# Routed and local attention on one core: token load order, routing logits, token-major local output, halved last sequence

## What is computed

```python
xn = layernorm(x)
s  = attn(xn, Wq, Wk, Wv)     # 8 heads, causal relu(QK^T)/512 times V, summed over heads, plus xn
g  = silu(ffn(xn, ...))
return x + s * g
```

```python
summed = scattered_routed_outputs + local_out
counts = (how many groups chose the token) + 1
ffn    = summed / counts
```

## Time and profile before

| | us |
|---|---|
| median of 3 runs | 774.32 (771.80 to 774.63) |
| the profiled execution | 774.42 |
| span of the profile, first to last instruction | 772.6 |
| PE busy | 732.4 (95%) |
| DVE busy | 478.3 (62%) |
| ACT busy | 420.8 (54%) |
| POOL busy | 222.7 (29%) |

### The profile page before, as it was taken

How to read it: one execution, slowest core, us unless ns; L and a number is a source line. 1 busy time by engine, 2 the same in 40 slices (tenths; PEclk the granted TensorE clock), 3 DMA queues, 4 the chain that set the end, 5 groups by cost and what they waited for, 6 DMA issues and landing times.

```text
span 772.6 us, 17339 instructions
## 1 busy us (share of the span) xinstructions
PE 732.4 (95%) x6062; PEld 563.2 (73%) x6068; DVE 478.3 (62%) x1076; ACT 420.8 (54%) x1527; POOL 222.7 (29%) x309
## 2 busy tenths in 40 slices
PE   4999999999999899999999999899999999999996
PEld 3678888878887566666666668778778777786875
DVE  5533333369886777777777775565665656656563
ACT  3344444432223577677766775465665746656572
POOL 3130000000003798776776741020312211001011
PEclk9999999999999999999999999899999999999999
DMA  8701000000001323333333330000000000000001
GB/s 248 290 1 56 0 0 0 0 0 0 2 0 35 94 65 75 86 89 83 87 83 91 80 93 2 1 12 8 17 4 14 10 8 2 0 0 0 0 1 56
DMA packets 26063, 32.69 MB, mean 42 GB/s; under 512 B 7056, under 2 KB 15760, under 8 KB 25360
## 3 DMA queue, kind: packets, MB, share of 16 engines
q1 hardware_dynamic: 24720, 29.25, 13.7%
q0 software_dynamic: 1280, 2.62, 1.3%
HBM read 12.98 MB, written 2.10 MB: 20 GB/s over the span
## 4 chain that ended last, share of the span: by engine, by line
PE 69%; DVE 10%; ACT 7%; issue 5%; POOL 3%; POOLq 2%; DVEq 2%; DMA 1%; SPq 1%; ACTq 0%
PE ps L735 9%; PE ps L747 9%; PE ps L999 7%; PE ps L1059 6%; PE ps L1026 4%; PE ps L1042 4%; PE ps L796 4%; PE ps L722 4%; PE ps L716 4%; ACT stage L1281 4%; DVE stage L1621 3%; PE ps L1035 2%; PE ps L920 2%; PE ps L906 2%; PE ps L868 2%
## 5 line engine op out<-in xcount | busy, mean ns | idle before, releaser
L562 POOL TENSOR_TENSOR early<-stage 128x512 f32<-128x512 f32 x64 | 87.9, 1394 | 56.1 <-DVE stage L1621 38.7
L1281 ACT ACTIVATE stage<-ps,nmB 128x128 f32<-128x128 f32 x256 | 89.9, 380 | 19.9 <-DVE nmB L1654 19.2
L1337 ACT ACTIVATE early<-ps,nmC 128x128 f32<-128x128 f32 (+1 forms) x224 | 77.6, 363 | 41.4 <-DVE dnC L1717 41.2
L747 PE MATMUL ps<-stage 128*128 128x128 f32 (+2 forms) x448 | 86.1, 321 | 1.4 <-DVE stage L1519 1.2
L735 PE MATMUL ps<-stage,early 128*128 128x128 f32 (+2 forms) x448 | 86.4, 321 | 0.0
L735 PEld LDWEIGHTS ps<-stage,early 128*128 128x128 f32 x448 | 65.2, 191 | 24.5 <-issue 15.5
L747 PEld LDWEIGHTS ps<-stage 128*128 128x128 f32 x448 | 65.5, 191 | 12.1 <-issue 1.9
L1026 PEld LDWEIGHTS ps<-stage,early 128*128 128x128 f32 x448 | 56.1, 193 | 23.5 <-issue 23.5
L1226 ACT ACTIVATE stage<-ps 128x512 f32<-128x512 f32 x64 | 31.4, 490 | 65.2 <-PE ps L735 65.2
L1042 PE MATMUL ps<-early,stage 128*128 128x512 f32 (+1 forms) x112 | 59.7, 615 | 4.2 <-ACT early L1349 4.2
L1712 DVE TENSOR_REDUCE nmC<-ps 128x4 f32<-128x512 f32 (+1 forms) x56 | 36.4, 650 | 44.0 <-PE ps L1026 43.9
(11 more groups left out here) (196 smaller groups left out, 1493.8 us busy)
## 6 DMA issues: line engine op xcount, KB each, us to landing
early<-early SPq DMA_DIRECT2D x256, 64.0 KB, 2.0
x<-in_x SPq DMA_DIRECT2D x4, 256.0 KB, 4.3
stage<-in_cq SPq DMA_DIRECT2D x1, 1024.0 KB, 7.9
stage<-in_ck SPq DMA_DIRECT2D x1, 1024.0 KB, 10.2
stage<-in_cv SPq DMA_DIRECT2D x1, 1024.0 KB, 11.9
stage<-in_co SPq DMA_DIRECT2D x1, 1024.0 KB, 14.1
early<-in_wqk SPq DMA_DIRECT2D x1, 1024.0 KB, 16.0
xrows<-xhat SPq DMA_DIRECT2D x1, 1024.0 KB, 5.2
```

The source lines that it names most:

```text
L562: pool.tensor_tensor(to, a, b, (ALU.subtract, ALU.add)[f]).then_inc(rot_in, 1)
L747: t = pe.matmul(ps[:, b, q0:q1], vN[:, b % 2, m, :], simA[:, b % 2, s, at:at + q1 - q0], start=False, stop=False, skip_group_check=True)
L1281: t = act.activation(pB[:, u % 2, at, :], ps[:, 4 + h, i * P:(i + 1) * P], ACT.Exp, bias=nmB[:, u % 2, at:at + 1], accum_out=rsB[:, u % 2, ...
L1337: act.activation(pC[:, k, hg, 0:n], ps[:, 5 + k, hg * P:hg * P + n], ACT.Exp, bias=nmC[:, k, hg:hg + 1], accum_out=rsC[:, k, hg:hg + 1])
```

## The change

It moves and replaces these things:

- SP loads all four token pieces first, then the score weights.
- One set of four products, of 72 rows and 512 columns, gives context logits and, for each group and sequence, the query logits of the whole sequence in 8 rows. DVE copies these to RU, and seven small SBUF to SBUF transfers on SP's queue spread them over the 56 rows. DVE's maximum moves behind the first tokens of the first head, and waits for these transfers.
- The transposes of the value weights move behind the logits, their copies on ACT behind the second inverse root.
- `b_out` takes the mixed values as the stationary operand, in four pieces of 128 tokens, so the local output has tokens in the rows. ACT scales it by `rcnt` while copying it to `loc`, in four pieces. POOL scales the 16 OHQ matrices by `rcnt` in the first sequence of stage C.
- `spread` has no products with the identity; DVE adds `loc` in the place of `mean`. The product by sN moves from POOL to DVE.
- In the last sequence, the turning, spread, addition, tanh, result and store go in two halves; DVE copies the second half of oN.

```diff
-        J_GA, J_WV, J_XNT, J_XLNT, J_END = 0, 2, 4, 8, 12
+        J_GA, J_XNT, J_WV, J_XLNT, J_END = 0, 2, 6, 8, 12
...
-            load_x(0)
-            load_x(1)
+            for b in range(B):
+                load_x(b)
             load_scores(0)
-            load_x(2)
-            load_x(3)
             load_scores(1)
...
+            sp.wait_ge(logits_in, 1)
+            for w in range(WQ):
+                sp.dma_start(RS[Q_AT + G * B * w:Q_AT + G * B * (w + 1), 0:W],
+                             RU[Q_AT:Q_AT + G * B, W * w:W * (w + 1)]).then_inc(s_spread, 16)
             sp.wait_ge(s_xhat, B)
...
+                        pool.wait_ge(qsel_out, B)
+                        for c in range(NB):
+                            at = OHQ[:, c, :]
+                            t = pool.tensor_scalar(at, at, rcnt[:, c % BLK, c // BLK:c // BLK + 1], None, ALU.mult)
+                        t.then_inc(ohq_scaled, 1)
-                pool.tensor_tensor(sN[:, b % 2].rearrange("p j n -> p (j n)"),
...
-                t = pe.matmul(ps[0:KV_ROWS, 1, 0:CTX], RTk[:, b, :], xnT[:, b, 0:CTX],
-                              start=(b == 0), stop=(b == B - 1))
+                t = pe.matmul(ps[0:RT_ROWS, 1, :], RT[:, b, :], xnT[:, b, :], start=(b == 0), stop=(b == B - 1))
             t.then_inc(logits, 1)
...
-            for w in range(WQ):
-                for b in range(B):
-                    t = pe.matmul(ps[Q_AT:Q_AT + Q_ROWS, 2, 0:W], RTq[:, w * B + b, :],
...
-                        pe.wait_ge(r_start, 1)
+                        pe.wait_ge(logits_in, 1)
...
-                pe.matmul(bank(7), bo[:, p, :], axB[:, u % 2, :], start=(p == 0), stop=(p == PAIRS - 1)).then_inc(out_done, 1)
+                for k in range(BLK):
+                    to = slice(k * P, (k + 1) * P)
+                    t = pe.matmul(ps[:, 7, to], axB[:, u % 2, to], bo[:, p, :], start=(p == 0 and k == 0),
+                                  stop=(p == PAIRS - 1), skip_group_check=True)
+                t.then_inc(out_done, 1)
...
-                    pe.matmul(ps[:, 5, to], OHS[:, b % 2, j, :], oN[:, b % 2, j, :], start=True, stop=False)
-                    t = pe.matmul(ps[:, 5, to], loc[:, b, to], ident[:], start=False, stop=True)
+                    t = pe.matmul(ps[:, 5, j * P:(j + 1) * P], OHS[:, b % 2, j, :], oN[:, b % 2, j, :], start=True, stop=True)
...
+            def last_turn(b):
+                pe.wait_ge(ft_in, 3 * b + 2)
+                for hf in range(2):
+                    for j in range(2):
+                        t = pe.transpose(ps[:, (6, 4)[hf], j * P:(j + 1) * P],
+                                         oT[:, b, 2 * hf + j].rearrange("p g s -> p (g s)"), ident[:])
+                    t.then_inc(ft_out, 1)
+            def last_spread(b):
+                pe.wait_ge(y_ready, b)
+                for hf in range(2):
+                    pe.wait_ge((ft_in, oN_half)[hf], (3 * b + 3, 1)[hf])
+                    for j in range(2):
+                        t = pe.matmul(ps[:, (5, 3)[hf], j * P:(j + 1) * P], OHS[:, b % 2, 2 * hf + j, :],
+                                      oN[:, b % 2, 2 * hf + j, :], start=True, stop=True)
+                    t.then_inc(fin_out, 1)
...
-                act.activation(loc[:, b, :], ps[:, 7, :], ACT.Copy).then_inc(loc_in, 1)
+                if b == 0:
+                    act.wait_ge(rcnt_in, 1)
+                for k in range(BLK):
+                    to = slice(k * P, (k + 1) * P)
+                    t = act.activation(loc[:, b, to], ps[:, 7, to], ACT.Copy, scale=rcnt[:, k, b:b + 1])
+                t.then_inc(loc_in, 1)
...
-            dve.wait_ge(logits, 2)
+            dve.wait_ge(logits, 1)
+            dve.tensor_copy(RU[qeach, :], ps[qeach, 1, W:N])
             dve.tensor_tensor(RS[0:KV_ROWS, :], ps[0:KV_ROWS, 1, 0:CTX], rmask[0:KV_ROWS, :], ALU.add)
-            dve.tensor_copy(RS[qrows, 0:W], ps[qrows, 2, 0:W])
-            dve.drain()
-            dve.tensor_reduce(rsmax[:], RS[:], AX.X, ALU.max)
             dve.memset(rm[:], 0.0)
-            dve.drain()
-            dve.nop().then_inc(r_start, 1)
+            dve.drain().then_inc(logits_in, 1)
...
+                        if b == 0:
+                            dve.wait_ge(s_spread, 16 * WQ)
+                            dve.tensor_reduce(rsmax[:], RS[:], AX.X, ALU.max)
+                            dve.drain().then_inc(r_start, 1)
...
-            for b in range(B):
-                k = b % 2
-                dve.wait_ge(e_ready, b + 1)
-                dve.wait_ge(sy_ready, b + 1)
-                dve.scalar_tensor_tensor(out=eN[:, k], in0=eN[:, k], scalar=1.0, in1=sN[:, k], op0=ALU.add, op1=ALU.mult)
-                if b + 2 < B:
-                    mean(b + 1)
...
+            gate_input(0)
+            null_turned(it)
+            for b in range(B - 1):
+                product(b)
+                result(b)
+                if b + 1 < B - 1:
+                    gate_input(b + 1)
+            b = B - 1
+            dve.wait_ge(ft_out, 3 * b + 4)
+            dve.tensor_copy(oN[:, b % 2, 2:], ps[:, 4, 0:2 * P].rearrange("p (j n) -> p j n", j=2)).then_inc(oN_half, 1)
+            gate_input(b, (0, 1))
+            product(b)
+            result(b, 0)
+            result(b, 1)
```

More of the change, by code:

```diff
@@ L207, in build @@
         ak, o = part(stage, o, [HA, D])
-        RTk, o = part(stage, o, [B, KV_ROWS])
-        RTq, o = part(stage, o, [WQ * B, Q_ROWS])
+        RT, o = part(stage, o, [B, RT_ROWS])
         o = 5120
@@ L503, in _, with diagonal @@
             pool.drain().then_inc(s_zero, 1)
-            pool.wait_ge(s_cleared, 4)
+            pool.wait_ge(s_cleared, 3)
             pool.wait_ge(s_rtw, 32)
-            flat = RTk.rearrange("p b r -> p (b r)")
+            flat = RT.rearrange("p b r -> p (b r)")
+            def diagonal(at, column):
+                return pool.tensor_copy(flat[:, at:at + (B - 1) * (RT_ROWS + 1) + 1:RT_ROWS + 1],
+                                        column.broadcast_to([P, B]))
             for w in range(KV_W0, WQ):
                 for g in range(G):
[L509 to L512, removed]
-            for w in range(WQ):
[L514 to L517, removed]
+                    diagonal(kv_row(w, g, 0), rtk[:, g:g + 1])
+            for g in range(G):
+                last = diagonal(Q_AT + g * B, rtq[:, g:g + 1])
             last.then_inc(s_rt, 1)
@@ L693, in _ @@
                 t.then_inc(prep_out, 1)
-            for w in range(WQ):
-                for b in range(B):
-                    t = pe.matmul(ps[Q_AT:Q_AT + Q_ROWS, 2, 0:W], RTq[:, w * B + b, :],
-                                  xnT[:, b, W * (w + 1):W * (w + 2)],
-                                  start=(w == 0 and b == 0), stop=(w == WQ - 1 and b == B - 1))
-            t.then_inc(logits, 1)
             pe.wait_ge(g_loaded, 1)
@@ L1168, in _ @@
             pe.wait_ge(cout_in, G * B)
-            turn_back(3, early=False)
-            spread(3)
+            last_turn(3)
+            last_spread(3)
         @block.scalar
@@ L1414, in exps, with last_exps @@
                 act.activation(eN[:, b % 2], yN[:, b % 2], ACT.Tanh).then_inc(e_ready, 1)
+            def last_exps(b):
+                act.wait_ge(res_in, b - 1)
+                for hf in range(2):
+                    half2 = slice(2 * hf, 2 * hf + 2)
+                    act.wait_ge(y_ready, b + 1 + hf)
+                    act.activation(eN[:, b % 2, half2], yN[:, b % 2, half2], ACT.Tanh).then_inc(e_ready, 1)
             it = LAST[2]
@@ L1429, in _ @@
             projected(*LAST)
-            turned_back(3, (2,))
-            exps(3)
+            act.wait_ge(ft_out, 3 * 3 + 3)
+            act.activation(oN[:, 1, 0:2], ps[:, 6, 0:2 * P].rearrange("p (j n) -> p j n", j=2), ACT.Copy).then_inc(ft_in, 1)
+            last_exps(3)
         @block.vector
@@ new lines, in product, with result @@
+            def product(b):
+                dve.wait_ge(ft_in, 3 * b + 2)
+                dve.drain()
+                dve.tensor_tensor(sN[:, b % 2], sN[:, b % 2], yN[:, b % 2], ALU.mult)
+                dve.drain()
+            def result(b, hf=None):
+                at = slice(0, BLK) if hf is None else slice(2 * hf, 2 * hf + 2)
+                dve.wait_ge(e_ready, b + 1 + (hf or 0))
+                dve.scalar_tensor_tensor(out=eN[:, b % 2, at], in0=eN[:, b % 2, at], scalar=1.0, in1=sN[:, b % 2, at],
+                                         op0=ALU.add, op1=ALU.mult)
+                dve.drain()
+                dve.tensor_tensor(res[:, b * BLK + at.start:b * BLK + at.stop, :], eN[:, b % 2, at],
+                                  x[:, b * BLK + at.start:b * BLK + at.stop, :], ALU.add).then_inc(res_in, 1)
```

60 lines of the change are left out of this document (30 added, 30 removed).

## The result

The changed kernel takes 768.07 us (median of 6 runs, 767.36 to 771.05) against 774.3 before (6 runs beside them): ratio 0.9936, 95% interval 0.992 to 0.9953. In a second series it took 766.8 (6 runs) against 773.23 (11 runs, one of them, of 847.1, left out of the ratio): 0.9915 (0.9893 to 0.9937). The ratios are estimated from all the single times, not from the two medians, so they can say a little less or more: 6.2 us by the medians of the first series, 5.0 by its ratio. The forecast was 769.2 in a range of 766.5 to 772.5.

A forecast was written before the change was run, and what follows sets the result against it. TensorE (PE), on the chain of waits for 69% of the span, was taken as the bound. Terms -1.6+0.5+0.5-4.5 = -5.1 from the profiled 774.42 gave 769.3, by the median 769.2; range 766.5 to 772.5 us.

The forecast's parts named there:

- start, with what is given back in stage A: Start: earlier tokens and 56 fewer small matmuls bring stage A's first product 2.2 earlier, 0.6 given back: -1.6 us.
- stage B: Local attention, 32 units: four 128-column output matmuls replace one, +0.03 where PE sets the pace, about half: +0.5 us.
- stage C: First sequence of routed attention: POOL's sixteen scalings just covered, DVE slowed beside POOL: +0.5 us.
- tail: After the last sequence: no identity products and a shorter way from last projection to last addition: -4.5 us.
- The identity products: Tail: three spreads before the last projection each lose four products of 0.22 on the chain: -2.67 us.
- The last segment: Tail, from end of last projection to last addition: 5.68 us instead of 7.53, -1.85.
- The rival of DVE as the bound: Tail: DVE becomes the bound and PE's 2.67 us go, total 771.9; chance 0.08.
- the start is given back: Start: the spread lands after 37.2 and ACT's wait eats all 2.2, total 770.8; chance 0.12.
- tokens no earlier: -0.8: Start: tokens land no earlier, so it gives -0.8 instead of -1.6 us; lies within the forecast, no chance of its own.
- The DVE price of +0.5: Stage C: four normalizations beside POOL and three on the chain, 4 x 0.12 = +0.5 us; rival +2.3, 771.0, chance 0.08.
- The cover: Stage C: POOL's sixteen scalings, 9.3 us, end at 507.3, before POOL's next copy at 508.23.
- The other side: Stage B: weight loads show by 0.23 in all 32 units, +7.4 instead of +0.5, total 776.1, slower; chance 0.06.

The follow-up runs named there:

- the one trace with the old order: The changed kernel with loads as before (two token pieces, two weight pieces, and so on): 770.15 us, ratio 0.9951 to the kernel before.
- the run that has them alone: The kernel before with only its output product of each stage B unit split into four parts of 128 columns: 773.71 us against 773.83, ratio 0.9998.
- the start alone: The kernel before with only tokens first, one logits product, seven transfers, DVE's copy and the later maximum: 771.79 us against 773.8, ratio 0.9969.
- both edits on POOL: The changed kernel with POOL's gather before its two rotary sums and the 32 column picks over eight units instead of four: 765.53 us, ratio 0.9887.
- the last sequence whole: The changed kernel with the last sequence handled in one piece with one store, not in halves: 768.13 us, ratio 0.9935 to the kernel before.
- the sums first: The changed kernel with POOL's two rotary sums put ahead of its two shifted copies: 770.82 us, ratio 0.9949 to the kernel before.
- sums held back: The changed kernel with POOL's two rotary sums waiting until DVE's second normalization is done: 773.43 us, ratio 1.0003 to the kernel before.
- gather ahead: The changed kernel with POOL's gather put ahead of its two rotary sums: 767.65 us, ratio 0.9924 to the kernel before.
- picks spread alone: The changed kernel with the 32 column picks over eight units instead of four, gathers unmoved: 771.68 us, ratio 0.9971 to the kernel before.
- the best kernel: The changed kernel plus both edits on POOL, stage A's first product not waiting for ACT's four copies, last weights issued behind the spread: 762.2 us, ratio 0.9856.

## Why the prediction was right, and where not

The two traces of the changed kernel make it possible to check the terms one by one against the trace of before.

| term | predicted (bounds) | first trace | second trace |
|---|---|---|---|
| start, with what is given back in stage A | -1.6 (-2.4, 0) | -2.65 | -2.87 |
| stage B | +0.5 (0, +2) | +4.04 | +0.38 |
| stage C | +0.5 (0, +2.3) | 0.00 | -0.08 |
| tail | -4.5 (-5.2, -3.7) | -4.94 | -4.95 |
| sum | -5.1 | -3.5 | -7.5 |

**Tail: right, two steps nearly to the hundredth.** The identity products: -2.67 predicted, -2.68 found (from the tail's beginning to the end of the last projection 18.64 instead of 21.32). The last segment: 5.68 predicted, 5.72 found, with half sums of 0.42 where I had estimated 0.42. What failed is the small step "the last transfer is taken as long as before": a store of half the size ends 2.26 after the last addition instead of 2.71, a gain of 0.45. The rival of DVE as the bound fell as its own numbers said, 15 us of room for 9.3 of work: from 742.42 to 761.08 the chain holds nothing but PE.

**Start: the sign and the parts right, the term too small, beyond its bound.** The first product came 2.9 earlier, not 2.2. The fourth token piece came 2.1 earlier, not 1.76, and with it the logits product ended at 20.37, not 20.7 to 21.2; that product took 3.65 as worked out (3.66), the transposes 0.87 (0.9). The spread landed at 34.8, not 35.6, well inside 33.4 to 36.2, and gave back 0.23 instead of 0.6; the rival "the start is given back" was wrong in size, but its mechanism is real, since the spread lands 2.5 earlier once the last weights stand behind it. The last of the rivals, "tokens no earlier: -0.8", was not tested cleanly: in the one trace with the old order the first product is 0.97 later than before, behind a logits product of 5.29 instead of 3.65; with passes as long as in the changed kernel it would be some 1.1 earlier than before by the estimate above.

**Stage B: the priced step was right, the term as measured first was not.** The output products cost 0.89 on the chain as forecast and 0.04 a unit where 0.03 was, the local copies nothing; in the second trace the term is +0.4. But the price of DVE standing beside POOL, which I had looked up for stage C, I did not carry to stage B, where both engines do the same thing 32 times. There the cost is no constant: it hangs on where POOL's sums fall against DVE's normalization, 0.28 or 1.1 us at a time, and on what POOL does meanwhile. It put 3.7 us between two traces of one kernel without any edit.

**Stage C: too careful, and the cover thinner than forecast.** POOL's sixteen scalings took 0.60 in the middle (0.58 predicted) and 10.0 together, not 9.3. In the first trace they ended at 509.53, just before 509.73 when POOL is next released; in the second, whose rows are the last two, POOL's next copy follows them without a pause, so there they were the later of the two:

```profile
499.53 10.00 POOL L645 TENSOR_SCALAR early<-early,rcnt 128x128 f32<-128x128 f32 x16
509.73 0.29 POOL L627 COPY stage<-xhat 128x128 f32<-128x128 f32 x1 [0.20 <-PE ps L1044]
...
495.46 10.22 POOL L645 TENSOR_SCALAR early<-early,rcnt 128x128 f32<-128x128 f32 x16
505.69 0.29 POOL L627 COPY stage<-xhat 128x128 f32<-128x128 f32 x1
```

The DVE price of +0.5 didn't appear; the four normalizations of that stretch take 0.42, 0.69, 0.69 and 0.71 in the first trace. The cover, forecast at 0.9 (507.3 against 508.23), was 0.2 there and nothing in the second; stage C lost nothing by it (-0.08).

**The other side**, weight loads at 0.23 in every unit, fell with the run that has them alone: 0.04.

The range held the time for a good reason in part (the tail) and in part by luck: the start's excess and what stage B loses by chance are of one size. Where stage B loses nothing, the sum is -7.5 and not -5.1; that run, 766.9, lies 0.4 above the lower end of the range, and of the six runs of the second series two lie below it.

## What to carry to other kernels

Where one engine's instruction takes longer beside another's (a normalization 0.97 and 1.80 instead of 0.69 here) and one of the two engines runs nearly as long per step as the other, their phase is not fixed: compare two traces of the same kernel, stage by stage, before a difference between two kernels is explained. A stretch of "issue" on an engine off the chain is worth a look, since a drain behind a gather made POOL's unit nearly as long as the others' here (6.6 to 6.8 us against 7.02), and moving the gather by one place helped only together with an evener load. Where a start comes later than worked out, compare the lengths of products of one shape over it, and not the view of the clock alone: here transposes took 0.42 and 0.27 with 1.00 in the view beside both. After an edit that moves a start, see what the first product really waits for: here 1.9 us stood in one wait for data that it didn't read.

## What the runs showed of the hardware that I had not expected

**A gather costs POOL more than its row.** The row takes 0.99 us, but the drain two instructions later waits another 1.25 to 2.72, mostly some 1.4; with two 1.25 us sums between gather and drain it waits 0.22. So in these traces the row alone understates what a gather takes.

**The clock fell behind short pauses, and not in every run.** In three further profiled runs with the new start (the start alone, both edits on POOL, the last sequence whole) and in that with the sums first, the second sequence of stage A follows the first by 5.1 to 5.2 us instead of 3.7, and stage A is 227.1 to 227.3 long instead of 225.8 to 226.3. The windows of the kernel with both edits on POOL (busy time of the engines, then granted clock, DMA share, GB/s):

```profile
26.00:28.00 2.00, 1.64 (x7) 1.64 (x8) 0.00 (x0) 0.31 (x1) 0.00 (x0) 0.59 1.02 430
28.00:30.00 2.00, 2.00 (x12) 2.00 (x11) 1.46 (x3) 0.00 (x0) 0.00 (x0) 0.55 1.01 426
30.00:32.00 2.00, 2.00 (x10) 1.18 (x9) 0.77 (x2) 0.80 (x2) 0.00 (x0) 1.00 0.98 408
```

PE had stood 1.93 us before its first product of stage A and 0.69 after it; then the granted clock was 0.59 and 0.55 in two windows of 2 us, which is as much as 0.50 for some 3.4 us. The changed kernel has the same pauses and kept 1.00 in both of its traces, as three more kernels with this start did in theirs (sums held back, gather ahead, picks spread alone); the best kernel, without the first pause, kept it in its one. At the entry to stage C the granted clock is down to 0.50 for several microseconds in each of the traces (480 to 487 us before, 482 to 488 in the changed kernel, 481 to 484 with the last sequence whole). In the first two it falls once more, from 504 to 508 and from 506 to 509. Stage C is 270.5 long in these two and 268.3 in the third. By these lengths that is a second chance effect of 1 to 2 us (an estimate), which no run here took away.
